# LSTM and sign-weight FFN on one core: reordering the sums of the last part over VectorE, ScalarE and GpSimd

## The chip, the cores and the metric

The kernel runs on one core of a Trainium2 chip. The time is the device time of one launch in microseconds (us), a median over runs. TensorE (PE) multiplies, VectorE (DVE), ScalarE (ACT) and GpSimd (POOL) do the elementwise work, SyncE (SP) issues most DMAs. The engines run their own instruction queues in order and wait for each other by semaphores only.

## The reference, cut to what matters

An LSTM over T = 64 steps, batch 32, input and hidden size 256, feeds an FFN whose weights are +1 or -1; its result is added to x.

```python
xW = einsum('ntd,dg->ntg', x, Wx) + b            # (32, 64, 1024)
for t in range(64):
    a = xW[:, t] + h @ Wh                        # (32, 1024): i, f, o, g
    c = sigmoid(f) * c + sigmoid(i) * tanh(g)
    h = sigmoid(o) * tanh(c)
h = concatenate([hs, -hs], -1)                   # (32, 64, 512)
h = relu(s0 * (h @ w0)) * 2                      # w0: 512 x 1024, +-1
h = relu(s1 * (h @ w1)) * 2                      # w1: 1024 x 1024, +-1
return x + s2 * (h @ w2)                         # w2: 1024 x 256, +-1
```

## The kernel before, in words

The LSTM steps form a serial chain: per step TensorE does 32 small matmuls against the high and low f16 parts of h (lines 485 and 494), VectorE sums the halves (line 1006), ScalarE takes the tanh (line 787), VectorE makes c and h (lines 1012 to 1026), and ScalarE seeds the next step's PSUM (line 676). What TensorE has left in a step is filled with other matmuls: first the input projection (tiles "x"), then the FFN of the steps that are done.

The FFN goes by chunks of steps: chunks 0 to 4 have 8 steps (256 columns), chunks 5 and 6 (N1 and N2) have 12 (384 columns). Layer 0 of chunk c gives eight tiles (0, c, m), layer 1 eight tiles (1, c, m), and the output is a sum over k of products ("o", c, k) in two PSUM banks ACC, one for each half mo. Values are held as a high and a low f16 part, so a drained tile costs one ScalarE operation (the high part, layer_hi) and one VectorE operation (the low part, layer_lo). The layer-1 parts lie in h2, a ring of NH2 = 6. When an output sum is complete, VectorE's y_add (line 860) scales it and adds it into x, and SP sends it out.

Layer 1 of chunks 5 and 6 together is done as a 2 x 2 block product with seven block multiplications instead of eight (Strassen's, in Winograd's form): q = 1 to 7, tiles ("p1", m) to ("p7", m), four m each, eight matmuls each. p2 is accumulated on p1, p6 on p5, p7 on p6, in the same PSUM bank. The weight combinations are mixed by GpSimd inside the loop (line 1078). The input combinations t1 to t4 need chunk 6 and are made behind the loop by n2_terms on VectorE (lines 879 to 884) and term4 on GpSimd (line 1089). Each is split in high (term_hi, ScalarE, line 731) and low part (term_lo: t_lo[0] and t_lo[3] on GpSimd, line 1082; t_lo[1] and t_lo[2] on VectorE, line 888). The product sums are: c11 = p1 + p2; q = p3 + p1, where ScalarE copies p3 out of PSUM (line 736) and GpSimd adds (line 1102); c12 = p6 + q (line 895); c22 = p7 + p1 (line 903); d = c22 - p5 on GpSimd (line 1106) after ScalarE's copy of p5 (line 743); c21 = p4 + d (line 910). c_rest (line 915) makes their low parts and c_split (line 752) the high ones. p7-m takes the bank of p6-m and so waits for c12_sum(m).

The order is written by a planner, make_plan, in Python. tile_order lists the matmuls of the loop in their order; a step t is given a credit fill(t) of 2.2 to 2.3 us, and matmuls are taken from the list by cost until it is spent or one is not ready (its inputs not emptied, or its bank not). act_plan[t] and dve_plan[t] hold what ScalarE and VectorE drain behind step t: VectorE gets at least two tiles a step, more if the planner's time (STEP, CHAIN, LOW, SUM) allows, and at most one y. tail_order puts what is left in order behind the loop. Per step ScalarE does its drains behind the second seed, VectorE behind line 1026.

Of the kernel before, what the change touches and what calls it, by code (L numbers as in the profile page):

```python
# [17 lines left out]
P = 128  # L18
# [4 lines left out]
NH2 = 6  # L23
# [35 lines left out]
STEP, CHAIN, CHAIN_MIN, LOW, SUM, AHEAD, KEEP = 0.87, 2.46, 2.87, 0.33, 0.40, 0.30, 0.05  # L59
# [33 lines left out]

def tile_order():
# [22 lines left out]

def tail_order(left):

    first_outs = [(tile, a) for tile, a in left if tile[0] == "o" and tile[1] == N1]  # L120
    left = [(tile, a) for tile, a in left if (tile, a) not in first_outs]
# [7 lines left out]
    order = [((0, N2, m + 4 * half), a) for m in range(4) for half in (0, 1) for a in range(4)] + left  # L129
    order += [(("p3", m), 2 * k + part) for k in range(4) for m in range(4) for part in (0, 1)]  # L130
    order += products(5, 0, 1) + first_outs + products(6, 0, 1) + products(7, 0, 1) + products(4, 0, 1) + products(5, 2, 3)
    order += outs(N2, 0, 1) + products(6, 2, 3) + outs(N2, 4, 5) + products(7, 2, 3) + outs(N1, 4, 5) + products(4, 2, 3)
    return order + outs(N2, 2, 3, 6, 7) + outs(N1, 6, 7)


def make_plan():
# [3 lines left out]
    pe, act, dve = ([[] for _ in range(T + 3)] for _ in range(3))  # L140
# [6 lines left out]
    ahead, waited = 0.0, 0  # L147

    def ready(tile, a, t):
# [6 lines left out]
        elif tile[0] == "p1":  # L156
            inputs = (0, N1, a // 2) in emptied
        elif tile[0] == "p2":
            inputs = (0, N1, 4 + a // 2) in emptied and ("p1", tile[1]) in emptied
        elif tile[1] == N1:  # L160
            inputs = ("p2", tile[2]) in emptied and ("y", N1 - 1, a // 2) in emptied
        else:
            inputs = (1, tile[1], tile[2]) in emptied
            inputs = inputs and (tile[1] == 0 or tile[2] > 0 or a > 0 or all(("y", tile[1] - 1, mo) in emptied for mo in range(2)))
# [11 lines left out]
    for t in range(-1, T):  # L176
        credit = min(credit, 1.0) + fill(t)
        finished, spent = [], 0.0
        while piece < len(order) and credit > 0.1:
# [3 lines left out]
            if not ready(tile, a, t):  # L183

                later = next((n for n in range(piece + 1, min(piece + AHEAD_O, len(order))) if order[n][0][0] == "o"), 0)
# [28 lines left out]
        for tile, at in finished:  # L214
            if tile[0] in ("x", "p1"):
                emptied.add(tile)
            if tile[0] != "y":
                act[t].append(tile)
# [4 lines left out]
        else:  # L223

            time = ahead + STEP + spent - CHAIN - KEEP - LOW * (t in W2_STEPS)
            lows, ys = ([x for x in todo if (x[0] == "y") == y] for y in (False, True))
            now = lows[:1 if ys and waited else max(2, int(time / LOW))]
            if ys and (len(now) < 2 or len(now) * LOW + SUM <= time):
                now.append(ys[0])
            waited = waited + 1 if ys and ys[0] not in now else 0  # L230
            ahead += STEP + spent - max(CHAIN_MIN, CHAIN + sum(SUM if x[0] == "y" else LOW for x in now))
            ahead = min(max(ahead, 0.0), AHEAD)
        act[t].sort(key=lambda x: x[0] == "x")
# [14 lines left out]
    for tile, a in tail_order(rest):  # L248
        free.sort(key=lambda b: empty_at[b[1]])
        if tile[0] == "o" and tile[1] == N2 and a == 0 and tile[2] == 0:  # L250
# [5 lines left out]
        if a + 1 == matmuls(tile) and tile[0] in (0, 1, "p2", "p3", "p4", "p7"):  # L256
            free.append((bank[tile], tile))
            empty_at[tile] = at + 1.2
            if tile[0] == 0 and tile[1] == N2:
                empty_at[tile] = 2.35 * (tile[2] % 4) + (1.5 if tile[2] < 4 else 3.3)  # L260
    finished = [tile for tile, a in pe[T] if a + 1 == matmuls(tile)]
    act[T] = [x for x in finished if x[0] in (1, "p1", "p2") or x[0] == 0 and x[1] == N1]
    for x in finished:
        if x[0] in (1, "p2") or x[0] == 0 and x[1] == N1:
            dve[T + 1].append(x)
        if x[0] == "o" and x[1] < N1 and x[2] == 7:
            dve[T + 1] += [("y", x[1], mo) for mo in range(2)]
    return pe, act, dve, bank, before


def lstm_ffn(nc, x_d, small_d, wx_d, wh_d, k0_d, k1_d, k2_d, out_d):
    ctx = ExitStack()
    with ctx:
# [26 lines left out]
        h1 = sb("h1", [P, 8192], F16)  # L300
        h2 = sb("h2", [P, NH2, 2, 512], F16)
# [29 lines left out]
        def cut(flat, first, *shape):  # L331
# [19 lines left out]
        h1s = [f.rearrange("p (m a c) -> p m a c", m=8, a=2) for f in (  # L351
            h1[:, 0:4096], h1[:, 4096:8192], h1[:, 0:4096], h1[:, 4096:8192], h1[:, 0:4096])] + [b1]
# [33 lines left out]
        acc_mm, y_made = ([sem(f"{n}{mo}") for mo in range(2)] for n in ("acc_mm", "y_made"))  # L386
# [5 lines left out]
        p3_made, q_made, p5_made, d_made = (sem(n) for n in ("p3_made", "q_made", "p5_made", "d_made"))  # L392
# [755 lines left out]
```

## Time and profile before

| | us |
|---|---|
| median of 3 runs (281.99 to 283.39) | 282.94 |
| profiled execution | 281.88 |
| its span | 279.9 |
| TensorE matmul busy | 269.1 (96%) |
| VectorE busy | 223.2 (80%) |
| ScalarE busy | 173.3 (62%) |
| GpSimd busy | 44.6 (16%) |

The span runs from the first to the last instruction of the profiled execution; the execution's own time also holds what lies around it. Matmul ends in the trace are modelled, so TensorE's busy share is not a share of its peak; starts are better to go by. A line of a timeline gives start, duration, engine, line, output and input, and in brackets how long the engine had been idle and what ended that. Consecutive operations of one engine overlap in part, so that the spacing of starts is shorter than a duration.

### The profile page before, as it was taken

To read this page: it belongs to the slowest core of one execution; us is meant where nothing else is said; L and a number is where in the kernel's file an instruction comes from. 1 tells how busy PE (TensorE), PEld (TensorE's weight loads), DVE (VectorE), ACT (ScalarE), POOL (GpSimd) and SP (SyncE) were. 2 spreads that over 40 slices of the span, in tenths; PEclk is the share of its full clock that TensorE was granted. 3 is DMA by queue.
4 is the path that set the end of the run, shared out by engine and by line. 5 is a ranking of instruction groups with operands and counts; after the bars stand their busy time and mean duration, and the time that the engine had idled before them with its cause. 6 is when DMAs were issued, how large, how long until landed. Compare 5 with 4: busy or idle time off the path is not lost.

```text
span 279.9 us, 8887 instructions
## 1 busy us (share of the span) xinstructions
PE 269.1 (96%) x3568; PEld 218.7 (78%) x3568; DVE 223.2 (80%) x777; ACT 173.3 (62%) x518; POOL 44.6 (16%) x62
## 2 busy tenths in 40 slices
PE   8999999999999999999999999999999996889995
PEld 6788878888999999999999988988878643446662
DVE  3888888888888888888888888878888877947355
ACT  4788887787565666556665565667766667443320
POOL 0110000011221111211112000000000030995030
PEclk9999999999999999999999999999999999999999
DMA  6970000000000000000000000000000000000003
GB/s 207 344 318 1 4 2 0 2 4 2 2 2 4 4 20 20 2 4 18 25 4 2 4 21 21 2 1 22 21 2 2 22 19 0 0 2 0 2 0 112
DMA packets 5432, 8.72 MB, mean 31 GB/s; under 512 B 656, under 2 KB 3472, under 8 KB 5264
## 3 DMA queue, kind: packets, MB, share of 16 engines
q1 hardware_dynamic: 5104, 7.64, 7.8%
q8 instruction: 28, 0.46, 0.6%
q10 hardware_dynamic: 288, 0.52, 0.5%
q14 instruction: 12, 0.10, 0.1%
HBM read 6.07 MB, written 2.10 MB: 29 GB/s over the span
## 4 chain that ended last, share of the span: by engine, by line
PE 72%; DVE 12%; ACT 8%; issue 4%; POOL 3%; DVEq 0%; POOLq 0%; ACTq 0%
PE WK L532 24%; PE WK L515 14%; PE G L494 8%; PE G L485 8%; PE WK L550 5%; PE ACC L564 4%; ACT tT L787 4%; PE G L550 2%; DVE aT L1006 2%; POOL xw L1082 2%; ACT tC L792 2%; DVE h L846 1%; DVE uT L1015 1%; DVE cD L1017 1%; DVE xw L846 1%
## 5 line engine op out<-in xcount | busy, mean ns | idle before, releaser
L532 PE MATMUL WK<-h,k 128*128 128x256 f16 (+1 forms) x848 | 106.3, 276 | 0.4 <-DVE h L1026 0.2
L532 PEld LDWEIGHTS WK<-h,k 128*128 128x128 fp8e5 x848 | 80.1, 98 | 11.7 <-issue 0.6
L787 ACT ACTIVATE tT<-aT 128x128 f32<-128x128 f32 x126 | 38.9, 310 | 49.3 <-DVE aT L1006 48.0
L1006 DVE TENSOR_REDUCE aT<-G 128x128 f32<-128x256 f32 x128 | 48.1, 418 | 4.1 <-PE G L494 2.8
L676 ACT ACTIVATE G<-xw 128x256 f32<-128x256 f32 x126 | 46.6, 370 | 0.0
L515 PE MATMUL WK<-xs,wxs 128*128 128x512 f32 x168 | 42.5, 399 | 0.0
L485 PEld LDWEIGHTS G<-h,w 128*128 128x128 f16 x1008 | 32.1, 96 | 9.6 <-DVE h L1023 8.2
L494 PE MATMUL G<-h,w 128*128 128x64 f16 x1008 | 39.5, 192 | 0.0
L485 PE MATMUL G<-h,w 128*128 128x32 f16 x1008 | 35.2, 177 | 1.1 <-DVE h L1023 1.0
L515 PEld LDWEIGHTS WK<-xs,wxs 128*128 128x128 f32 x168 | 30.4, 188 | 5.9
L494 PEld LDWEIGHTS G<-h,w 128*128 128x128 f16 x1008 | 33.2, 97 | 0.0
L846 DVE SCALAR_TENSOR_TENSOR h<-WK,h 128x256 f16<-128x256 f32 x80 | 30.9, 417 | 0.0
L792 ACT ACTIVATE tC<-cD 128x64 f32<-128x64 f32 x64 | 16.4, 256 | 17.6 <-DVE cD L1017 17.6
L695 ACT ACTIVATE h<-WK 128x256 f16<-128x256 f32 x80 | 26.6, 369 | 0.2
L1023 DVE TENSOR_TENSOR h<-oP,tC 128x64 f16<-128x64 f32 x64 | 14.4, 225 | 13.9 <-ACT tC L792 13.9
L1078 POOL TENSOR_TENSOR mix<-k 128x256 fp8e5<-128x256 fp8e5 x16 | 10.3, 644 | 78.0 <-DVE h L1026 78.0
L564 PE MATMUL ACC<-h,k 128*128 128x256 f16 x160 | 22.7, 273 | 0.0
L1082 POOL TENSOR_TENSOR xw<-w,xw 128x384 f16<-128x384 f32 x8 | 8.5, 1073 | 82.0 <-ACT xw L731 82.0
L1015 DVE SCALAR_TENSOR_TENSOR uT<-tT,cD 128x64 f32<-128x64 f32 x63 | 14.2, 226 | 6.5
L550 PE MATMUL WK<-xw,k 128*128 128x384 f16 x96 | 17.1, 326 | 1.9 <-ACT xw L700 1.9
L668 ACT ACTIVATE xw<-WK,biasS 128x512 f32<-128x512 f32 x28 | 18.1, 678 | 0.4 <-PE WK L515 0.4
L1012 DVE SCALAR_TENSOR_TENSOR vT<-tT 128x64 f32<-128x64 f32 x63 | 14.2, 226 | 2.9
(116 smaller groups left out, 301.8 us busy)
## 6 DMA issues: line engine op xcount, KB each, us to landing
x<-in_x SPq DMA_DIRECT2D x3, 512.0 KB, 8.4
out_y<-x SPq DMA_DIRECT2D x10, 128.0 KB, 1.8
xw<-in_wh SPq DMA_DIRECT2D x4, 256.0 KB, 5.2
k<-in_k SPq DMA_DIRECT2D x1, 1024.0 KB, 10.2
out_y<-x SPq DMA_DIRECT2D x4, 192.0 KB, 1.9
x<-in_x ACTq DMA_DIRECT2D x2, 256.0 KB, 3.4
xw<-in_wx SPq DMA_DIRECT2D x4, 128.0 KB, 4.3
xw<-in_wx SPq DMA_DIRECT2D x2, 256.0 KB, 5.5
```

The source lines that it names most:

```text
L485: eng.matmul(G[g][:, 64 * (j - j0):64 * (j - j0) + B], w16[:, 1, j, k], hi[:, k], start=False, stop=False, skip_group_check=True)
L494: ins = eng.matmul(G[g][:, 64 * (j - j0):64 * (j - j0 + 1)], w16[:, 0, j, k], pair[:, k].rearrange("p a b -> p (a b)"), start=False, stop= ...
L515: ins = eng.matmul(TILE[bank[tile]][:, :], wxs[:, wp, k, j], xs[:, i % 2, xp, k], start=a == 0, stop=a == 5)
L532: ins = eng.matmul(layer_src(tile), w, rhs, start=a == 0, stop=last)
L550: ins = eng.matmul(layer_src(tile), w[:, k, 128 * m:128 * m + 128], rhs[:, k, part], start=a == 0 and q not in (2, 6, 7), stop=a == 7, ski ...
L564: ins = eng.matmul(ACC[mo][:, 0:width(tile)], w2[:, k, 128 * mo:128 * mo + 128], h2[:, k % NH2, part, 0:width(tile)], start=k == 0 and par ...
L676: eng.activation(G[g][:, 0:256].rearrange("p (j h b) -> p j h b", h=2, b=B), src.unsqueeze(2).broadcast_to((P, 4, 2, B)), ACT.Copy, scale= ...
L695: eng.activation(layer_dst(tile, 0), layer_src(tile), ACT.Relu).then_inc(hi_made[layer])
L787: eng.activation(tT[:, B * j0:B * j1], aT[:, j0:j1].rearrange("p j b -> p (j b)"), ACT.Tanh, scale=half_gain0 if t == 0 else half_gain).th ...
L792: eng.activation(tC[:, :, :].rearrange("p j b -> p (j b)"), cD[:, :], ACT.Tanh, scale=0.5).then_inc(c_tanh)
L846: eng.scalar_tensor_tensor(layer_dst(tile, 1), layer_src(tile), 0.0, layer_dst(tile, 0), ALU.max, ALU.subtract).then_inc(lo_made[tile[0]])
L1006: eng.tensor_reduce(aT[:, j0:j1], G[g][:, 0:256].rearrange("p (j h b) -> p j b h", h=2, b=B), op=ALU.add, axis=AX.X).then_inc(added[g])
```

## The change

- t_lo[3] moves from GpSimd to VectorE, and so does q = p3 + p1 (q_sum), which now reads p3 out of PSUM; ScalarE's copy of p3 goes away. t1 and t4 get four slots instead of two, and the waits for their reuse go.
- The output products of chunk 4 (("o", 4, k), 32 matmuls) are no longer in the loop's order but behind it: ten of them first, the others between the layer-0 tiles of chunk 6. The outputs of chunk 5, k = 0 to 3, follow these tiles. h2 has eight places instead of six ring places.
- The output sums of chunks 0 to 3 are scaled and copied out of PSUM by ScalarE (y_copy) and added into x by GpSimd a step later. Chunk 4's are added by VectorE behind the second n2_terms. GpSimd's mixing is put into a loop over the steps.
- The planner has a cost for VectorE by width instead of LOW and SUM, and the last outputs of chunk 5 are ordered by half.

```diff
 def tile_order():
...
-            order += [(("o", c, k), 4) for k in range(6) if at_o[k] == m] + third(c, m)
-
-    order += [(("o", N1 - 1, 6), 4), (("p1", 0), 8), (("o", N1 - 1, 7), 4), (("p1", 1), 8), (("p2", 0), 8), (("p2", 1), 8),
-              (("p1", 2), 8), (("p1", 3), 8), (("p2", 2), 8), (("p2", 3), 8)]
-    return order + [(("o", N1, k), 4) for k in range(4)]
+            if c < N1 - 1:
+                order += [(("o", c, k), 4) for k in range(6) if at_o[k] == m]
+            order += third(c, m)
+
+    return order + [((f"p{q}", m), 8) for q, m in ((1, 0), (1, 1), (2, 0), (1, 2), (2, 1), (1, 3), (2, 2), (2, 3))]
...
 def tail_order(left):
-    order = [((0, N2, m + 4 * half), a) for m in range(4) for half in (0, 1) for a in range(4)] + left
+    others = outs(N1 - 1, *range(8))
+    order = left + others[:10]
+    for k, n in enumerate((6, 8, 8, 0)):
+        order += [((0, N2, k + 4 * half), a) for half in (0, 1) for a in range(4)] + others[:10 + n][10:]
+        del others[10:10 + n]
+    order += outs(N1, 0, 1, 2, 3)
     order += [(("p3", m), 2 * k + part) for k in range(4) for m in range(4) for part in (0, 1)]
-    order += products(5, 0, 1) + first_outs + products(6, 0, 1) + products(7, 0, 1) + products(4, 0, 1) + products(5, 2, 3)
+    order += products(5, 0, 1) + products(6, 0, 1) + products(7, 0, 1) + products(4, 0, 1) + products(5, 2, 3)
     order += outs(N2, 0, 1) + products(6, 2, 3) + outs(N2, 4, 5) + products(7, 2, 3) + outs(N1, 4, 5) + products(4, 2, 3)
-    return order + outs(N2, 2, 3, 6, 7) + outs(N1, 6, 7)
+    order += outs(N2, 2, 3, 6, 7)
+    return order + [(("o", N1, k), 2 * mo + part) for mo in range(2) for k in (6, 7) for part in range(2)]
...
 def make_plan():
-            lows, ys = ([x for x in todo if (x[0] == "y") == y] for y in (False, True))
-            now = lows[:1 if ys and waited else max(2, int(time / LOW))]
-            if ys and (len(now) < 2 or len(now) * LOW + SUM <= time):
-                now.append(ys[0])
+            now = []
+            for x in todo:
+                if len(now) < 2 or sum(map(vector_cost, now + [x])) <= time:
+                    now.append(x)
...
         def _(eng):  # ScalarE
+            def y_copy(tile):
+                _, c, mo = tile
+                e.wait_ge(acc_mm[mo], c + 1)
+                e.wait_ge(signed, 6)
+                e.wait_ge(y_made[mo], c)
+                eng.activation(ty[:, mo], ACC[mo][:, 0:width(tile)], ACT.Copy, scale=FAC).then_inc(y_out[mo])
...
+            for tile in act_plan[T]:
+                empty(tile)
             for k in range(4):
                 n2_relu(k)
                 n2_hi(k)
                 term_hi(0, k)
                 term_hi(1, k)
-            for tile in act_plan[T]:
-                empty(tile)
-            for i, k in ((3, 0), (3, 1), (2, 0), (2, 1), (2, 2), (2, 3), (3, 2), (3, 3)):
-                term_hi(i, k)
-            for m in range(4):
-                p3_copy(m)
+            for i in (2, 3):
+                for k in range(4):
+                    term_hi(i, k)
...
         def _(eng):  # VectorE
+            def q_sum(m):
+                e.wait_ge(prod_mm[3], m + 1)
+                e.wait_ge(p1_made, m + 1)
+                e.wait_ge(t_made[0], 4)
+                eng.tensor_tensor(qs[:, m], layer_src(("p3", m)), p1s[:, m], ALU.add).then_inc(q_made)
...
             for k in range(4):
                 n2_terms(k)
-            for tile in dve_plan[T + 1]:
-                empty(tile)
+                if k == 1:
+                    for mo in range(2):
+                        y_add(N1 - 1, mo)
             for i in (1, 2):
                 for k in range(4):
                     term_lo(i, k)
+            for m in range(4):
+                q_sum(m)
+            for k in range(4):
+                term_lo(3, k)
...
         def _(eng):  # GpSimd
-            for n in range(MIXES):
-                mix_part(n)
+            def y_add(c, mo):
+                at = x[:, mo, steps_of(c)]
+                eng.wait_ge(y_out[mo], c + 1)
+                eng.tensor_tensor(at, at, ty[:, mo], ALU.add).then_inc(y_made[mo])
+
+            for t in range(T):
+                if 0 <= t - MIX_STEP < MIXES:
+                    mix_part(t - MIX_STEP)
+                for _, c, mo in pool_plan[t]:
+                    eng.wait_ge(hl_made, t + 1)
+                    y_add(c, mo)
             for k in range(4):
                 term_lo(0, k)
-                if k >= 1:
-                    term_lo(3, k - 1)
                 term4(k)
-            term_lo(3, 3)
-            for m in range(4):
-                eng.wait_ge(p3_made, m + 1)
-                eng.wait_ge(p1_made, m + 1)
-                eng.tensor_tensor(qs[:, m], qs[:, m], p1s[:, m], ALU.add).then_inc(q_made)
```

## Rows read from the trace of the kernel before

**Rows 1.** Busy by engine from 100 to 200 us: stretch, length, engines, clock, DMA.

```profile
100.00:200.00 100.00, 99.33 (x1645) 89.89 (x1644) 85.27 (x340) 62.44 (x214) 10.91 (x17) 1.00 0.04 13
```

**Rows 2.** Timeline of VectorE's h product, loop steps 16, 40, 43 and 62.

```profile
72.93 0.22 DVE L1023 TENSOR_TENSOR h<-oP,tC 128x64 f16<-128x64 f32 x1 [0.22 <-ACT tC L792]
...
149.46 0.22 DVE L1023 TENSOR_TENSOR h<-oP,tC 128x64 f16<-128x64 f32 x1 [0.22 <-ACT tC L792]
...
159.14 0.22 DVE L1023 TENSOR_TENSOR h<-oP,tC 128x64 f16<-128x64 f32 x1 [0.21 <-ACT tC L792]
...
221.63 0.23 DVE L1023 TENSOR_TENSOR h<-oP,tC 128x64 f16<-128x64 f32 x1 [0.22 <-ACT tC L792]
```

**Rows 3.** Timeline of TensorE's matmuls behind the loop.

```profile
225.88 1.46 PE L532 MATMUL WK<-h,k 128*128 128x384 f16 x8 [0.24 <-DVE h L1026]
...
229.45 0.82 PE L532 MATMUL WK<-h,k 128*128 128x384 f16 x4 [0.17 <-DVE xw L884]
...
231.64 0.82 PE L532 MATMUL G<-h,k 128*128 128x384 f16 x4 [0.69 <-DVE xw L884]
232.30 1.79 PE L550 MATMUL WK<-xw,k 128*128 128x384 f16 x10
236.02 1.47 PE L550 MATMUL WK<-xw,k 128*128 128x384 f16 x8 [1.93 <-ACT xw L700]
...
245.69 0.48 PE L550 MATMUL WK<-xw,mix 128*128 128x384 f16 x2 [2.02 <-POOL xw L1082]
...
250.51 1.48 PE L550 MATMUL WK<-xw,mix 128*128 128x384 f16 x8 [0.45 <-ACT xw L743]
...
253.13 1.46 PE L550 MATMUL WK<-xw,mix 128*128 128x384 f16 x8
```

**Rows 4.** Timeline of VectorE behind the loop.

```profile
227.25 0.56 DVE L879 SCALAR_TENSOR_TENSOR w<-WK,xw 128x384 f32<-128x384 f32 x1 [1.05 <-ACT xw L723]
...
229.44 0.56 DVE L879 SCALAR_TENSOR_TENSOR w<-G,xw 128x384 f32<-128x384 f32 x1
...
235.41 0.55 DVE L884 SCALAR_TENSOR_TENSOR xw<-G,xw 128x384 f16<-128x384 f32 x1
...
238.53 9.89 DVE L888 TENSOR_TENSOR xw<-t,xw 128x384 f16<-128x384 f32 x8
...
252.03 0.56 DVE L895 TENSOR_TENSOR w<-WK,xw 128x384 f32<-128x384 f32 x1 [3.61 <-PE WK L550]
...
276.40 1.14 DVE L860 SCALAR_TENSOR_TENSOR x<-ACC,sc,x 128x384 f32<-128x384 f32 x2 [0.16 <-PE ACC L581]
```

**Rows 5.** Timeline of GpSimd behind the loop.

```profile
228.44 0.92 POOL L1082 TENSOR_TENSOR xw<-w,xw 128x384 f16<-128x384 f32 x1 [74.12 <-ACT xw L731]
...
243.03 1.32 POOL L1089 TENSOR_TENSOR w<-xw,t 128x384 f32<-128x384 f32 x1
...
249.51 3.86 POOL L1102 TENSOR_TENSOR xw<-xw 128x384 f32<-128x384 f32 x4
```

**Rows 6.** Timeline of ScalarE behind the loop.

```profile
248.04 0.52 ACT L731 ACTIVATE xw<-w 128x384 f16<-128x384 f32 x1 [3.12 <-POOL w L1089]
...
249.95 0.51 ACT L743 ACTIVATE xw<-WK 128x384 f32<-128x384 f32 x1
```

**Rows 7.** Timeline of VectorE before the loop, GpSimd idle.

```profile
16.48 2.06 DVE L837 SCALAR_TENSOR_TENSOR w<-xw,sci,w 128x512 f16<-128x512 f32 x3
```

**Rows 8.** Chain of waits (start, duration, what), and one group of lines.

```profile
151.42 0.87 PE ACC L564 x8
...
222.88 0.39 DVE x L860
...
L695 ACT ACTIVATE h<-WK 128x256 f16<-128x256 f32 x80 | 26.6, 369 | 0.2
```

More of the change, by code:

```diff
@@ L91, in cost, with vector_cost @@
     return 0.229 if tile[0] == "x" else 0.000422 * width(tile)
+def vector_cost(tile):
+    return 0.05 + 0.0011 * width(tile)
 def tile_order():
@@ L159, in ready @@
             inputs = (0, N1, 4 + a // 2) in emptied and ("p1", tile[1]) in emptied
-        elif tile[1] == N1:
-            inputs = ("p2", tile[2]) in emptied and ("y", N1 - 1, a // 2) in emptied
         else:
             inputs = (1, tile[1], tile[2]) in emptied
-            inputs = inputs and (tile[1] == 0 or tile[2] > 0 or a > 0 or all(("y", tile[1] - 1, mo) in emptied for mo in range(2)))
+            first = tile[1] > 0 and tile[2] == 0 and a == 0
+            inputs = inputs and (not first or all(("y", tile[1] - 1, mo) in emptied for mo in range(2)))
         return inputs and (before.get(tile) is None or before[tile] in emptied)
@@ L183, in make_plan @@
             if not ready(tile, a, t):
-                later = next((n for n in range(piece + 1, min(piece + AHEAD_O, len(order))) if order[n][0][0] == "o"), 0)
+                instead = ("o", 1) if tile[0] == 0 and a == 0 else ("o",)
+                later = next((n for n in range(piece + 1, min(piece + AHEAD_O, len(order))) if order[n][0][0] in instead), 0)
                 if not later or tile[0] == "o" or not ready(order[later][0], done.get(order[later][0], 0), t):
@@ L249, in make_plan @@
         free.sort(key=lambda b: empty_at[b[1]])
-        if tile[0] == "o" and tile[1] == N2 and a == 0 and tile[2] == 0:
+        if tile == ("o", N2, 0) and a == 0:
             for mo in range(2):
@@ L258, in make_plan @@
             empty_at[tile] = at + 1.2
[L259 to L268, printed above, removed]
+            if tile[0] == 0:
+                empty_at[tile] = 1.6 + 2.2 * (tile[2] % 4) + (1.7 if tile[2] < 4 else 3.4)
+    act[T] = [tile for tile, a in rest if a + 1 == matmuls(tile)]
+    dve[T] += [tile for tile in act[T] if tile[0] != "p1"]
+    return pe, act, dve, pool, bank, before
 def lstm_ffn(nc, x_d, small_d, wx_d, wh_d, k0_d, k1_d, k2_d, out_d):
@@ L349, in lstm_ffn @@
         a11, a21, a12, a22 = (w1[:, 4 * j:4 * j + 4, 512 * i:512 * i + 512] for j in range(2) for i in range(2))
[L351 to L352 removed]
+        h1s = [cut(h1[:, c % 2], 0, 8, 2, B * CHUNKS[c][1]) for c in range(N1)] + [b1]
         G = [pb("G0"), pb("G1")]
@@ L391, in lstm_ffn @@
         t_made, t_hi, t_lo = ([sem(f"{n}{i}") for i in range(4)] for n in ("t_made", "t_hi", "t_lo"))
[L392 removed]
+        q_made, p5_made, d_made = (sem(n) for n in ("q_made", "p5_made", "d_made"))
         c_sum, c_hi, c_lo = ({q: sem(f"{n}{q}") for q in (11, 12, 21, 22)} for n in ("c_sum", "c_hi", "c_lo"))
[L394 to L396 removed]
+        fin_mm, fin_y = ({c: [sem(f"{n}{c}_{mo}") for mo in range(2)] for c in (N1 - 1, N1, N2)} for n in ("fin_mm", "fin_y"))
+        pe_plan, act_plan, dve_plan, pool_plan, bank, before = make_plan()
         def layer_dst(tile, part):
[L399 removed]
+            return h1s[tile[1]][:, tile[2], part] if tile[0] == 0 else h2[:, tile[2], part, 0:width(tile)]
         def layer_src(tile):
@@ L404, in term @@
         def term(i, k):
-            return (t1f[:, k % 2], t23[:, 0, k], t23[:, 1, k], t4f[:, k % 2])[i]
+            return (t1f, t23[:, 0], t23[:, 1], t4f)[i][:, k]
         def steps_of(c):
@@ L456, in _ @@
             eng.dma_start(k2[:, :], k2_d).then_inc(dk2, 16)
-            for c in range(N1):
+            for c in range(N1 - 1):
                 for mo in range(2):
@@ L562, in out_matmul @@
                 elif k == 0:
-                    e.wait_ge(y_made[mo], c)
+                    e.wait_ge(y_out[mo], c)
                 ins = eng.matmul(ACC[mo][:, 0:width(tile)], w2[:, k, 128 * mo:128 * mo + 128],
-                                 h2[:, k % NH2, part, 0:width(tile)], start=k == 0 and part == 0, stop=k == 7 and part == 1)
+                                 h2[:, k, part, 0:width(tile)], start=k == 0 and part == 0, stop=k == 7 and part == 1)
                 if k == 7 and part == 1:
@@ L711, in empty @@
                     p1_copy(tile)
+                elif tile[0] == "y":
+                    y_copy(tile)
                 elif tile[0] == "p2":
```

76 lines of the change are left out of this document (30 added, 46 removed).

## The prediction

> **What bounds the kernel now.** I read the busy time by stretches first, then the starts of the h product, which mark the 64 steps of the loop, then TensorE's timeline behind the loop, and last what VectorE, GpSimd and ScalarE do there. Inside the loop the reader is to see a full TensorE: 99.33 us of matmul in the 100 us from 100 to 200, at a granted clock of 1.00 [rows 1]. The 24 steps between the starts at 72.93 and 149.46 take 76.53 us, 3.19 each; the 19 between 159.14 and 221.63 take 62.49, 3.29 each [rows 2]. So the late steps lose 0.10 us each, 1.9 in all, against the earlier ones that hold the same amount of planned filler.
>
> Behind the loop TensorE is not full. It starts the tail at 225.88, the first half product of group 6 (p6-0) at 250.51 and the first of group 7 (p7-0) at 253.13 [rows 3]; from 250.51 on nothing keeps it waiting until the end. Before 250.51 the waits in front of its rows are 0.24, 0.17, 0.69, 1.93, 2.02 and 0.45 us, 5.5 in all. The first three belong to the layer-0 tiles of the last chunk (hl of the last step, then PSUM banks not yet drained by line 884), the fourth to p2-3, whose bank waits for ScalarE's line 700 copy of p1-3, queued behind the n2 operations; the fifth to t_lo[0] from GpSimd (line 1082); the sixth to ScalarE's copy of p5-0 (line 743).
>
> The last two have one root. GpSimd holds 16 operations in line there: 8 of line 1082, 4 of line 1089, 4 of line 1102. A line-1082 subtraction takes 0.92 us alone, one of line 1089 takes 1.32 while VectorE also works SBUF to SBUF, and the four q sums start only at 249.51 [rows 5]. ScalarE cannot go on to p3 and p5 before GpSimd's last t4: it idles 3.12 us before 248.04 and does p5-0 at 249.95 [rows 6]. VectorE meanwhile takes 9.89 us for eight subtractions of line 888, 1.24 each [rows 4].
>
> **The change, part by part.** The sum goes along TensorE, from the end of the loop's matmuls (225.88 - 0.24 = 225.64) to the start of p6-0, since behind p6-0 the order is the old one.
>
> *Matmuls behind the loop.* Before there were 114 of 384 columns: 32 of the last chunk's layer 0, 18 left of p1 and p2, 32 of p3, 16 of p5, 16 outputs of chunk 5. Sixteen start in 253.13 - 250.51 = 2.62 us, 0.163 each [rows 3]: 18.6 us. With the waits of 5.5 that is 24.1; the rows have 250.51 - 225.64 = 24.9, since a wait is counted from a group's modelled end, 0.16 us behind its last start, five times. After, 32 output matmuls of chunk 4, 256 wide, come in. Eight of those take 0.87 us [rows 8], so 32 take 3.5. The 18 leftovers (2.9 us) should go into the loop, where the 3.5 us of chunk 4's outputs make room: the planner hands out the same credit. Then the tail up to p6-0 is 96 x 0.163 + 3.5 = 19.1 us, and a tail without waits starts p6-0 at 244.8, 5.7 us earlier.
>
> *Do waits come back?* Engine by engine, by the spacings of the rows. Ten chunk-4 output matmuls (1.1 us) run first and cover the last hl; they need nothing of the last step. The first layer-0 tile then starts at 226.75, and VectorE follows 1.37 us behind, as 227.25 follows 225.88 [rows 3, 4]: 228.1. One group of n2 terms takes 2.19 us (229.44 - 227.25). Two end at 232.5; then VectorE waits for the last chunk-4 output. Before that stand 32 x 0.109 + 24 x 0.163 = 7.4 us of matmuls: 233.0. Its two adds at 0.39 [rows 8] end at 233.9, and terms 2 and 3 at 238.3. TensorE puts the other chunk-4 products between the layer-0 tiles, so that each bank has its 2.2 us to drain; the chunk-5 outputs start at 234.3 and need the adds of 233.9; p3 runs 236.9 to 242.1 and needs the last b22 at 238.3. The first four waits, 3.0 us, are covered.
>
> *GpSimd.* Its queue is now t_lo[0] and t4, four times each. The last t1 is ready at about 236.7, its high part at 237.3, so t_lo[0] ends at 238.2 and t4 at 239.2. p5 needs them at 242.1: the wait of 2.02 is gone with 2.9 us to spare. ScalarE, no longer holding the p3 copies, ends term_hi at 241.2 and takes p5-0 (done at 243.4) by 244.1, before 244.8: the wait of 0.45 is gone.
>
> *VectorE inherits the queue.* Between 238.3 and p7-0 it has eight subtractions of line 888, the four q sums out of PSUM, four more subtractions (t_lo[3]) and then c12_sum(0), for which p7-0 waits because it takes p6-0's bank. This is the dear spot. No row shows a 384-wide SBUF-to-SBUF subtraction on VectorE with GpSimd idle. Bounds: 1.24 us, line 888 itself beside GpSimd [rows 4]; and 0.47, the shortest spacing of the n2 operations, from 230 to 235, of which 235.41 is the last [rows 4]. The nearest row is three line-837 operations of 512 columns from SBUF, 2.06 us with GpSimd idle, starts 0.66 apart [rows 7]; by columns alone that is 0.50 for 384. I take 0.53, since part of a duration is fixed, and 0.9 for the first, which meets GpSimd's last t4. So: 238.3 + 0.9 + 7 x 0.53 = 242.9; q sums at 0.49, 244.9; t_lo[3], 247.0; c12_sum(0), 0.56, 247.6. TensorE asks for it at 244.8 + 2.6 = 247.4. A wait of 0.2 to 0.3 comes back. Tail: 5.7 - 0.3 = 5.4 us.
>
> The row first: beside GpSimd line 888 takes 1.24 us, and a sum reading PSUM (252.03) takes 0.56 though GpSimd's q sums run beside it [rows 4, 5]. The Trainium skill, page "SBUF — State Buffer", section "Who interferes with whom", says the same as a rule: VectorE with two SBUF inputs and GpSimd reading SBUF exclude each other for a whole instruction; VectorE with at most one SBUF input is free. Where this speaks against the change is rival two.
>
> *The loop.* Ten y adds of 0.39 us [rows 8] leave VectorE inside the loop (eight go to ScalarE and GpSimd, two behind the loop). Per mean step that is nothing, since TensorE is the limit there; it counts in the late steps, where VectorE's backlog of low parts delays tiles and the chain. Of their 1.9 us [rows 2] I credit 1.0: bounds 0 (the extra belongs to the 384-wide tiles, which stay) and 1.9. The 0.5 us of loop filler less (3.5 - 2.9) is worth 0.2: a step already near its chain length cannot shrink by all of it; bounds 0 and 0.5. The eight added ScalarE copies are 0.37 us each by the 256-wide rows [rows 8] and lie behind the two seeds, where ScalarE idles before the next tanh; cover gone, they would cost 8 x 0.3. GpSimd's adds start behind hl, when VectorE reads PSUM. The mixes keep their steps. The output DMAs of chunk 4 go out at 234 on SP, in front of nothing that waits; below and above zero I see no price. The buffers t1f and t4f with four slots take away waits that no row shows to bind: 0.
>
> *The end.* The last output halves are put so that mo 0 is complete four matmuls before the end, not two. Now both last adds wait in one row, 1.14 us from 276.40 [rows 4]; one of them moves under the matmuls, less 0.3 because the adds overlap in the queue: 0.2 gained; bounds 0 and 0.5.
>
> Sum: 5.4 + 1.0 + 0.2 + 0.2 = 6.8 us. The profiled execution took 281.88 us (span 279.9), so 275.1. The median of the three runs, 282.94, lies 1.06 above it; I forecast 276.1 for the median.
>
> **The rivals.** *One: the loop does not take the leftovers.* The four WK banks and the low parts of chunk 5 can hold p2 back; a step with nothing ready still costs its chain, 3.06 us or so. One product of eight matmuls left over adds 1.3 us behind the loop, and the loop's own 1.2 is not gained: 276.1 + 2.5 = 278.6. For it: such holes are seen in the late steps. Against: the y adds that leave stand in VectorE's queue there, one of them on the chain at 222.88 [rows 8].
>
> *Two: the GpSimd adds meet the h chain.* Lines 1012 to 1026 are VectorE operations with two SBUF inputs. A 256-wide add, two thirds of 0.92, would hold one back by up to 0.6; eight times, 4.8: 280.9. For it: line 888 beside GpSimd. Against: an add that starts right behind hl ends before the next vT, some 1.4 us later; only two adds behind a mix reach it. The skill's rule ("the loser fully blocks", page "SBUF — State Buffer") gives this same case.
>
> *Three, slower: the subtraction costs VectorE 1.24 us by itself*, GpSimd or not. Then 238.3 + 8 x 1.24 + 2.0 + 4 x 1.24 + 0.56 = 255.7 for c12_sum(0), and p7-0 starts 2.6 us later than before; less the 1.4 of loop and end, 282.94 + 1.2 = 284.1. It decides from 1.14 us a piece. For it: each of the eight is slow, and its second input is f16. Against: GpSimd was busy beside nearly all of them, and line 837, f16 output, is not slow.
>
> *Four: something between*, 0.8 us a piece: p7-0 late by 3.3 more, 279.4.
>
> **How the numbers follow.** Forecast 0.62; one 0.18; two 0.07; three 0.06; four 0.07. Left open at either side, the range 274.0 to 279.8 holds the forecast's own band, one and four. No change within 0.5% (1.4 us, about what a measurement of this kernel tells) means 281.5 to 284.4: part of three and the upper edge of two, 0.05; slower 0.05; faster 0.90.
>
> **What would show it.** p6-0 near 243.5 and no TensorE wait over 0.5 us between the loop's end and it; line 888 at about 0.55 to 0.6 us once GpSimd's t4 is done; GpSimd done with t4 before p3 ends; c12_sum(0) within 0.5 us of p6-0's end; late steps at 3.2 us. Wrong if line 888 stays above 1 us with GpSimd idle, if p2 matmuls stand in front of the chunk-4 outputs behind the loop, or if the h chain's lines grow beside the new adds.

## The result, and the profile after

The changed kernel takes 275.89 us (median of 4 runs, 275.60 to 276.26); the kernel before, on the same chips, 282.63 (4 runs, 281.99 to 283.39). The ratio is 0.976, with a 95% interval from 0.973 to 0.979: faster, by 6.7 us. The forecast was 276.1, with a range of 274.0 to 279.8.

The profiled executions took 281.88 and 275.96 us, 5.9 apart; the spans 279.9 and 274.2. All splits below are made inside the spans.

The medians lie further apart (6.7) than the profiled executions (5.9). Part of that goes with TensorE's clock. The kernel before was run 32 more times beside the experiments. In 11 of these runs the granted clock, averaged over the span, was 1.00, and the times are 281.80 to 282.67 us (median 282.26); in 12 it was 0.992 to 0.994, and the times are 282.74 to 283.37 (median 283.00). All four runs of the changed kernel show 1.00. So some 0.4 us (282.63 - 282.26) of the 6.7 go with a clock that only the kernel before lost. Its profiled execution is one with a clock of 1.00, so no trace shows where it was lost.

First the page of the profile after: busy time (share of the span, instructions) and the shares of the chain of waits.

```profile
PE 268.8 (98%) x3568; PEld 219.2 (80%) x3568; DVE 219.3 (80%) x777; ACT 174.3 (64%) x522; POOL 40.7 (15%) x62
...
PE 85%; DVE 7%; ACT 5%; DMA 1%; issue 1%; ACTq 0%
```

TensorE is as busy as before, 268.8 us against 269.1, in a span 5.7 us shorter. The work is nearly the same and idle time is gone. The next view is TensorE's timeline behind the loop (start, busy time, line, count, and in brackets any wait ahead of the row). It answers to [rows 3].

```profile
225.90 1.26 PE L565 MATMUL ACC<-h,k 128*128 128x256 f16 x10
226.99 1.46 PE L533 MATMUL WK<-h,k 128*128 128x384 f16 x8
228.29 0.82 PE L565 MATMUL ACC<-h,k 128*128 128x256 f16 x6
...
234.59 2.76 PE L582 MATMUL ACC<-h,k 128*128 128x384 f16 x16
237.19 0.81 PE L551 MATMUL WK<-xw,mix 128*128 128x384 f16 x4
...
242.39 7.80 PE L551 MATMUL WK<-xw,mix 128*128 128x384 f16 x47
```

No row carries a bracket. The chunk-4 outputs (128x256, line 565) stand first and between the layer-0 tiles. The last row, cut at 250, holds 47 of the 48 matmuls of the first halves of p5, p6 and p7, without a break, where the kernel before waited 2.02 us for GpSimd and 0.45 for ScalarE. Sixteen matmuls of p5 at 0.163 put p6-0 at 242.39 + 2.61 = 245.00. From the end of the loop's matmuls to p6-0 the kernel before needed 250.51 - 225.64 = 24.9 us; this one needs 245.00 - 225.90 = 19.1, which is 5.8 less.

The engines that feed it come next: VectorE (answers to [rows 4]), then the single rows of GpSimd and ScalarE (to [rows 5, 6]).

```profile
233.28 0.88 DVE L862 SCALAR_TENSOR_TENSOR x<-ACC,sc,x 128x256 f32<-128x256 f32 x2 [0.41 <-PE ACC L565]
...
238.32 4.66 DVE L885 TENSOR_TENSOR xw<-h,xw 128x384 f16<-128x384 f32 x8
242.90 1.01 DVE L891 TENSOR_TENSOR xw<-WK,xw 128x384 f32<-128x384 f32 x2
...
244.76 1.95 DVE L885 TENSOR_TENSOR xw<-w,xw 128x384 f16<-128x384 f32 x4
246.63 0.54 DVE L898 TENSOR_TENSOR t1f<-WK,xw 128x384 f32<-128x384 f32 x1
```

```profile
238.32 1.43 POOL L1097 TENSOR_TENSOR w<-xw,h 128x384 f32<-128x384 f32 x1
```

```profile
243.89 0.49 ACT L746 ACTIVATE xw<-WK 128x384 f32<-128x384 f32 x1 [2.56 <-PE WK L551]
```

VectorE's eight subtractions (line 885, line 888 before) take 4.66 us instead of 9.89. GpSimd's last t4 ends at 239.75, well ahead of p5 at 242.39. ScalarE, which idled for GpSimd before, now waits for TensorE alone and has p5-0 copied at 244.4, before p6-0 starts.

The loop, by TensorE's first group of line 486 and by the start of VectorE's h product (line 1026; the first and the second pair answer to those of [rows 2]):

```profile
19.49 0.56 PE L486 MATMUL G<-hz,w 128*128 128x32 f16 x16
```

```profile
73.23 0.23 DVE L1026 TENSOR_TENSOR h<-oP,tC 128x64 f16<-128x64 f32 x1 [0.22 <-ACT tC L795]
...
150.36 0.22 DVE L1026 TENSOR_TENSOR h<-oP,tC 128x64 f16<-128x64 f32 x1 [0.22 <-ACT tC L795]
...
160.04 0.22 DVE L1026 TENSOR_TENSOR h<-oP,tC 128x64 f16<-128x64 f32 x1 [0.22 <-ACT tC L795]
...
222.88 0.22 DVE L1026 TENSOR_TENSOR h<-oP,tC 128x64 f16<-128x64 f32 x1 [0.22 <-ACT tC L795]
```

The 24 early steps take 77.13 us (76.53 before), the 19 late ones 62.84 (62.49 before). The loop is no faster: from that first group to the tail it is 225.90 - 19.49 = 206.41 us, against 206.43 before, where the same group (then line 485) started at 19.21. The 0.28 us by which the loop starts later is in no edit; it differs from run to run (19.00 and 19.57 in two experiments with the same code there).

This zero hides two things that cancel. The last group of this line marks the last step, first after, then before:

```profile
223.25 0.56 PE L486 MATMUL G<-h,w 128*128 128x32 f16 x16
```

```profile
222.33 0.55 PE L485 MATMUL G<-h,w 128*128 128x32 f16 x16
```

From the first group to the last it is 203.76 us, against 203.12 before: 0.64 longer. From the last group to the tail it is 2.65 us, against 3.31, because the plan gives the last step 11 filler matmuls instead of 14. (The 225.64 of the kernel before is a modelled end. By the spacing of the starts it lies 0.16 us earlier, which would move 0.16 us of gain from the loop to the tail.)

At the end, the last matmuls and the last adds:

```profile
269.69 1.46 PE L582 MATMUL ACC<-h,k 128*128 128x384 f16 x8
```

```profile
270.63 1.18 DVE L862 SCALAR_TENSOR_TENSOR x<-ACC,sc,x 128x384 f32<-128x384 f32 x2
```

The adds end 271.81 - 271.15 = 0.66 us behind the matmuls; before it was 0.85. So the span's 5.7 us are 5.8 (tail) + 0.0 (loop) + 0.2 (end) - 0.3 (the later start).

### The profile page after: what moved, and what is told of

It is laid out like the page before. It is cut to its first block, busy times and chain, and to the rows that moved or that the text cites. A ratio compares the mean times of both kernels' runs of the same rounds, so it can differ in the third digit from the quotient of the medians.

```text
span 274.2 us, 8895 instructions
## 1 busy us (share of the span) xinstructions
PE 268.8 (98%) x3568; PEld 219.2 (80%) x3568; DVE 219.3 (80%) x777; ACT 174.3 (64%) x522; POOL 40.7 (15%) x62
## 4 chain that ended last, share of the span: by engine, by line
PE 85%; DVE 7%; ACT 5%; DMA 1%; issue 1%; ACTq 0%
PE WK L533 27%; PE WK L516 14%; PE G L495 10%; PE WK L551 9%; PE G L486 9%; PE ACC L565 6%; PE G L551 4%; PE WK L582 2%; ACT tT L790 2%; DVE aT L1009 2%; PE ACC L582 1%; DMA x<-in_x 1%; PE G L516 1%; DVE xw L848 1%; ACT xw L688 1%; PE ACC L516 1%
## 5 line engine op out<-in xcount | busy, mean ns | idle before, releaser
L533 PE MATMUL WK<-h,k 128*128 128x256 f16 (+1 forms) x856 | 107.7, 276 | 0.0
L565 PE MATMUL ACC<-h,k 128*128 128x256 f16 x160 | 22.0, 273 | 0.0
L565 PEld LDWEIGHTS ACC<-h,k 128*128 128x128 fp8e5 x160 | 15.3, 98 | 2.1
```

What stands on the lines that cost most here:

```text
L533: ins = eng.matmul(layer_src(tile), w, rhs, start=a == 0, stop=last)
L565: ins = eng.matmul(ACC[mo][:, 0:width(tile)], w2[:, k, 128 * mo:128 * mo + 128], h2[:, k, part, 0:width(tile)], start=k == 0 and part == 0 ...
```

## The experiments

Two questions: what makes the tail's 5.8 us, and why the loop gives nothing. The ratio is against the kernel before, run beside it. The diffs are cut to what matters; three dots stand for lines left out.

| kernel | median us | ratio, 95% interval |
|---|---|---|
| changed kernel | 275.89 | 0.976 (0.973 to 0.979) |
| e1_queue_back | 284.37 | 1.006 (1.004 to 1.008) |
| e10_queue_back_warm | 281.70 | 0.997 (0.996 to 0.998) |
| e2_split_alone | 279.09 | 0.988 (0.986 to 0.990) |
| e11_pool_busy | 283.82 | 1.005 (1.003 to 1.008) |
| e9_t0_on_vector | 276.77 | 0.979 (0.977 to 0.980) |
| e4_y_on_vector | 276.27 | 0.979 (0.977 to 0.981) |
| e5_y_spread | 274.99 | 0.974 (0.972 to 0.975) |
| e6_lag | 275.74 | 0.976 (0.974 to 0.978) |
| e7_spread_lag | 274.88 | 0.973 (0.972 to 0.975) |
| e12_spread_lag2 | 274.34 | 0.971 (0.970 to 0.973) |

### The order without the split: e1_queue_back

The changed kernel with the last part's queues as before: t_lo[3] and the q sums on GpSimd, the p3 copies on ScalarE.

```diff
 VectorE:
-            for m in range(4):
-                q_sum(m)
-            for k in range(4):
-                term_lo(3, k)
...
 ScalarE:
+            for m in range(4):
+                p3_copy(m)
...
 GpSimd:
                 term_lo(0, k)
+                if k >= 1:
+                    term_lo(3, k - 1)
                 term4(k)
+            term_lo(3, 3)
+            for m in range(4):
...
+                eng.tensor_tensor(qs[:, m], qs[:, m], p1s[:, m], ALU.add).then_inc(q_made)
```

> The changed kernel with one part undone: t_lo[3] and the q sums are GpSimd's again, with ScalarE's copy of p3; the outputs of chunk 4 stay behind the loop. Theory A (the two parts of the tail need each other): GpSimd's queue ends its last t_lo[0] at about 245.6 us as before, p5 waits some 2.5 us for it, and ScalarE's copy of p5-0 lies behind the p3 copies at about 250, with no chunk-5 outputs left to cover it; p6-0 starts near 250.3 instead of 245.0 and the time is 281.2 (280.5 to 281.9), so nearly the whole gain is gone. Rival B (the parts add up): only the waits of 2.02 and 0.45 us before p5 and p6 come back, 278.4 us. Rival C (the gain is the order alone): 276 us.

Measured 284.37, slower than the kernel before and above all three forecasts. TensorE's timeline of this run:

```profile
245.90 2.84 PE L551 MATMUL WK<-xw,mix 128*128 128x384 f16 x10 [2.38 <-POOL xw L1094]
...
250.74 8.29 PE L551 MATMUL WK<-xw,mix 128*128 128x384 f16 x32 [2.00 <-ACT xw L751]
```

Both old waits are back and the second is longer (2.00 for 0.45), because the matmuls that used to stand between p5 and p6 (chunk 5's first outputs) now run earlier. That is the expected part (p6-0 at 250.74, forecast 250.3). What theory A missed is in the stretches (length, then busy time of PE, PEld, DVE, ACT, POOL, then the granted clock as the number ahead of the last two):

```profile
244.00:245.00 1.00, 0.00 (x0) 0.00 (x0) 1.00 (x2) 0.40 (x1) 1.00 (x2) 1.00 0.00 0
...
247.00:248.00 1.00, 1.00 (x5) 0.48 (x4) 0.36 (x1) 0.00 (x0) 1.00 (x1) 0.50 0.00 0
...
255.00:256.00 1.00, 1.00 (x5) 0.49 (x4) 0.00 (x0) 0.00 (x0) 0.00 (x0) 0.50 0.00 0
...
257.00:258.00 1.00, 1.00 (x8) 0.61 (x7) 0.88 (x3) 0.20 (x1) 0.00 (x0) 1.00 0.00 0
```

After the idle time the granted clock is 0.50 (1.2 GHz) and five matmuls run in a microsecond; at 257 it is 1.00 (2.4 GHz) again, with eight. The kernel before, behind its wait of 2.02 us at the same place, shows no such fall in its profiled execution:

```profile
246.00:247.00 1.00, 1.00 (x9) 0.60 (x7) 1.00 (x1) 0.00 (x0) 1.00 (x2) 1.00 0.00 0
```

### The same with TensorE kept busy: e10_queue_back_warm

```diff
             def matmul(tile, a):
+                if tile == ("p5", 0) and a == 6:
+                    warm_up(("p5", 1), 22)
+                if tile == ("p6", 0) and a == 0:
+                    warm_up(("p4", 0), 12)
...
```

warm_up issues that many 256-wide matmuls of zeros into the bank that the named tile fills later.

> The kernel with GpSimd's queue put back (284.37 us), with 22 matmuls of zeros, 256 wide, in the wait ahead of p5's last part and 12 in the wait ahead of p6-0, each into a PSUM bank that is free; they keep TensorE at work and release nothing. Theory F (about 3 us of that kernel's loss are TensorE at half its clock, granted 0.50 from about 246.5 to 256.4, after an idle stretch of 2.38 us): the clock stays 1.00 and the time is 281.3 (280.8 to 281.9). Rival G (the loss is waits alone): 284.4 or more.

Measured 281.70. The stretch from 240 to 260 us, at a clock of 1.00, and the timeline of TensorE:

```profile
240.00:260.00 20.00, 18.42 (x124) 11.64 (x122) 13.61 (x18) 8.58 (x19) 15.18 (x14) 1.00 0.00 1
```

```profile
243.28 2.56 PE L612 MATMUL WK<-zero 128*128 128x256 f16 x22
...
249.17 1.48 PE L612 MATMUL WK<-zero 128*128 128x256 f16 x12 [1.54 <-ACT xw L753]
250.69 5.37 PE L551 MATMUL WK<-xw,mix 128*128 128x384 f16 x32
```

p6-0 starts at 250.69, as in e1 (250.74), and its 32 matmuls take 5.37 us instead of 8.29. So 2.7 us of e1 are the clock (284.37 - 281.70, by the medians; e1's runs differ, with mean clocks of 0.982 and 0.994), and the queues as they were cost 281.70 - 275.89 = 5.8 us by their waits alone.

### The split without the order: e2_split_alone

The kernel before, with only the engines changed: VectorE takes t_lo[3] and the q sums (straight from PSUM), ScalarE loses the p3 copies, and the buffers of t1 and t4 get four slots.

> The kernel before with one part of the change: t_lo[3] and the q sums on VectorE, t1 and t4 with four slots, no p3 copies; order, planner and y adds are those of before. Theory A: the bank waits behind the loop (0.17, 0.69, 1.93 us) stay, the waits of 2.02 and 0.45 us go, p6-0 starts near 247.8 instead of 250.5: 2.7 us less than before, about 280.0 (279.4 to 280.6). Rival B (only the order counts): 282.6. Rival C (the engine split is the whole gain): under 278.

Measured 279.09, 0.3 below theory A's range; the rivals are refuted. TensorE's rows that answer to [rows 3]:

```profile
226.42 1.46 PE L536 MATMUL WK<-h,k 128*128 128x384 f16 x8 [0.25 <-DVE h L1027]
...
236.57 1.47 PE L554 MATMUL WK<-xw,k 128*128 128x384 f16 x8 [1.94 <-ACT xw L704]
...
248.28 1.46 PE L554 MATMUL WK<-xw,mix 128*128 128x384 f16 x8
```

and VectorE's subtractions, which answer to line 888 of [rows 4]:

```profile
239.08 3.83 DVE L883 TENSOR_TENSOR xw<-t,xw 128x384 f16<-128x384 f32 x8
```

The waits behind GpSimd are gone and those of the last chunk's banks stay (1.94 for p2-3). From first tail matmul to p6-0 it is 21.9 us, 24.6 before. The eight subtractions take 3.83 us where they took 9.89: 0.47 each with GpSimd idle. So the split alone is worth 3.4 us by the ratio, of which the tail up to p6-0 shows 2.8; some of the rest is the clock again, which was 1.00 in all four runs of e2. The rest of the change without the split loses (e1), or gains 0.3% where the clock is kept up (e10), and both together bring 6.7. The order needs the split, for it takes away the products that covered GpSimd's queue.

### GpSimd kept busy: e11_pool_busy

The changed kernel, with ten 384-wide SBUF-to-SBUF adds on GpSimd behind the last t4, whose results nobody reads.

```diff
+            for n in range(10):
...
+                eng.tensor_tensor(k0[:, 1, 0:NW].bitcast(F32), p1s[:, 0], p1s[:, 1], ALU.add).then_inc(mixed)
```

> The changed kernel with ten more 384-wide adds on GpSimd, SBUF to SBUF, behind its last t4; nothing waits for them. Theory H (a VectorE subtraction with two SBUF inputs takes 0.47 us alone and about 1.24 beside GpSimd): VectorE's eight subtractions take 9.5 us instead of 4.6, the q sums out of PSUM stay at 0.47, c12_sum(0) comes near 253.3 instead of 246.6 and p7-0 waits 5 to 6 us; with the clock lost after such a gap 283 to 285.5 us. Rival I (VectorE's line 888 was slow before for another reason): 275.9.

Measured 283.82, as theory H has it. VectorE, GpSimd and TensorE of this run:

```profile
238.09 9.46 DVE L885 TENSOR_TENSOR xw<-h,xw 128x384 f16<-128x384 f32 x8
247.47 1.01 DVE L891 TENSOR_TENSOR xw<-WK,xw 128x384 f32<-128x384 f32 x2
```

```profile
239.48 12.53 POOL L1117 TENSOR_TENSOR k<-xw 128x384 f32<-128x384 f32 x10
```

```profile
253.42 4.36 PE L551 MATMUL WK<-xw,mix 128*128 128x384 f16 x16 [5.89 <-DVE t1f L898]
```

The subtractions are back at 1.18 each, while the sums that read PSUM keep their 1.01 for two. GpSimd's adds take 1.25 each, against 0.96 for its four q sums with VectorE idle (3.86 in [rows 5]). The price of 1.24 in [rows 4] is thus GpSimd's work beside VectorE, not the subtraction's own. The Trainium skill, page "SBUF — State Buffer", section "Who interferes with whom", has as a rule that a VectorE instruction with two SBUF inputs contends with a GpSimd instruction that reads SBUF, and that one with at most one SBUF input does not. The trace agrees with both halves: 1.18 against 0.47 us for the subtractions, and 1.01 for two of the sums that read PSUM here as in the changed kernel.

### How near VectorE's queue is: e9_t0_on_vector

```diff
 VectorE:
-            for i in (1, 2):
+            for i in (0, 1, 2):
                 for k in range(4):
                     term_lo(i, k)
...
 GpSimd:
-                term_lo(0, k)
```

> The changed kernel with the four t_lo[0] subtractions moved from GpSimd to VectorE too, ahead of its others. Theory J (VectorE's queue behind the loop is the nearest next bound: c12_sum(0) ends at 247.2 us, p7-0 starts at 247.6, some 0.45 us of room): four times 0.47 us more, less 0.4 for the first subtraction that no longer meets GpSimd, make c12_sum(0) 1.5 us later and p7-0 1.0 to 1.1 us later: 276.9 us (276.5 to 277.4). Rival K (VectorE has room for 2 us): 275.9.

Measured 276.77, 0.9 us more, as theory J has it. The intervals of the ratios touch, but its four runs (276.38 to 277.18) lie above the four of the changed kernel. TensorE:

```profile
248.79 2.77 PE L551 MATMUL WK<-xw,mix 128*128 128x384 f16 x16 [0.64 <-DVE t1f L898]
```

p7-0 now waits for c12_sum(0), the place that the prediction called the dear spot. Four more subtractions (1.9 us, less GpSimd's interference with the first one) turn a small margin into a wait of 0.64.

### The loop: e4_y_on_vector

The changed kernel with the y adds of chunks 0 to 3 back on VectorE inside the loop.

```diff
-            if tile[0] == "y":
-                pool[t + 1].append(tile)
-            act[t].append(tile)
+            if tile[0] != "y":
+                act[t].append(tile)
...
```

> The changed kernel with the y sums of chunks 0 to 3 undone: VectorE adds them out of PSUM inside the loop again, with the new planner costs; nothing else is different. Theory A (moving them off VectorE cost time): the long steps 27 and 36 (vT held back beside GpSimd's adds, 0.2 us each beyond the filler) and 53 (seven ScalarE operations ahead of the tanh, 0.7 us) go, a half-full step at 44 comes: 275.2 us (274.7 to 275.7). Rival B (as predicted, the move is worth about 1 us in the late steps): 276.9. Rival C: no difference, 275.9.

Measured 276.27, ratios 0.979 and 0.976 with overlapping intervals: by the medians the move is worth 0.4 us, less than rival B's 1 us, and theory A, that it costs time, is refuted. By the steps of the profile it does take something away. The extra time of a step is here its length less its planned filler and 0.865 us. Over the loop it sums up to 6.4 us in e4 and 5.7 in the changed kernel, of which 0.03 a step, some 1.9, stands in steps without any loss. The kernel before has 5.0, and the places differ: before, steps 45, 51 and 58 mostly (0.57, 0.47, 0.53); after, steps 27 (0.22), 36 (0.26) and 53 to 60 (0.71 in 53). Old losses went, new ones came. The changed kernel's rows show three causes.

In step 27 (and 36), two GpSimd adds behind a mix:

```profile
105.85 0.64 POOL L1088 TENSOR_TENSOR mix<-k 128x256 fp8e5<-128x256 fp8e5 x1 [2.52 <-DVE h L1029]
106.45 1.41 POOL L1102 TENSOR_TENSOR x<-x,t1f 128x256 f32<-128x256 f32 x2
```

```profile
103.95 0.23 DVE L1015 SCALAR_TENSOR_TENSOR vT<-tT 128x64 f32<-128x64 f32 x1
...
107.22 0.72 DVE L1015 SCALAR_TENSOR_TENSOR vT<-tT 128x64 f32<-128x64 f32 x1
```

vT, on the h chain, takes 0.72 instead of 0.23. In step 53 the chain waits for ScalarE instead:

```profile
190.73 0.87 ACT L723 ACTIVATE t1f<-ACC,sc 128x256 f32<-128x256 f32 x2
```

```profile
191.83 0.23 DVE L1015 SCALAR_TENSOR_TENSOR vT<-tT 128x64 f32<-128x64 f32 x1 [0.74 <-ACT tT L790]
```

Both y copies stand behind five other ScalarE operations and ahead of the step's tanh (tT). In e4 the same step loses 0.8 us, because both y adds stand on VectorE ahead of the reduction aT:

```profile
190.88 0.87 DVE L861 SCALAR_TENSOR_TENSOR x<-ACC,sc,x 128x256 f32<-128x256 f32 x2
191.66 0.75 DVE L1010 TENSOR_REDUCE aT<-G 128x128 f32<-128x256 f32 x2
```

So the move of the y adds carried the obstruction of this step from one engine to the other. In steps 55 to 60 the cause is the chain of waits (start, duration, engine, what):

```profile
203.26 0.41 ACT xw L688
203.67 0.39 ACT xw L694
204.06 0.02 issue
204.08 0.56 DVE xw L848
204.64 0.34 DVE aT L1009
```

VectorE has no backlog there any more, so it takes the low part of a layer-0 tile (line 848) in the step in which ScalarE makes its r1 copy and high part (688, 694), and the reduction aT of the h chain stands behind it. In the plan of the kernel before VectorE drained these tiles a step after ScalarE. That lag is gone in e4 too, where steps 55 to 59 have the same extra time as after, 1.5 us. So it is the new order and the planner's new costs that took it away, and not the move of the y adds; no run separates these two from each other.

### The y work spread over steps: e5_y_spread

```diff
-                pool[t + 1].append(tile)
-            act[t].append(tile)
+                pool[t + 2 + tile[2]].append(tile)
+                act[t + 1 + tile[2]].append(tile)
+            else:
+                act[t].append(tile)
```

> The changed kernel with the two y sums of a chunk spread over two steps: the copy of half 0 is ScalarE's one step later, that of half 1 two steps later, GpSimd's adds a step behind each. Theory A: one add (0.71 us) behind a mix (0.64) ends before the next vT, so vT stays at 0.23 us in all steps, and step 53 loses its overfull ScalarE: 1.0 us less than the changed kernel, 274.9 us (274.5 to 275.4). Rival B (the two-add steps are hidden by TensorE's filler): 275.9.

Measured 274.99, 0.9 us less than the changed kernel, as expected. The intervals of the ratios overlap, but all five runs (274.47 to 275.23) lie below the four of the changed kernel. The same spot as above in this run:

```profile
109.25 0.72 POOL L1104 TENSOR_TENSOR x<-x,t1f 128x256 f32<-128x256 f32 x1
```

```profile
109.90 0.23 DVE L1017 SCALAR_TENSOR_TENSOR vT<-tT 128x64 f32<-128x64 f32 x1
```

One add a step ends before vT starts and vT keeps its 0.23. The extra time falls from 5.7 to 4.7 us; step 53 from 0.71 to 0.14.

### VectorE one step behind: e6_lag, e7_spread_lag and e12_spread_lag2

e6 lets VectorE drain chunk 5's layer-0 tiles a step later; e7 is e5 and e6 together.

```diff
-                (late if spent - at < 0.75 else todo).append(tile)
+                (late if spent - at < 0.75 or tile[:2] == (0, N1) else todo).append(tile)
```

> The changed kernel with one change in the planner: VectorE drains the layer-0 tiles of chunk 5 a step later than ScalarE, as its old backlog did, not in the same step. Theory D (the steps 55 to 60 are 0.13 to 0.37 us longer than their filler because VectorE waits for ScalarE's high part of the same step and its reduce comes late): these extras go, 1.2 to 1.5 us less than the changed kernel, 274.5 us (274.1 to 275.0); two steps get less full. Rival E (the two 384- and 256-wide drains by themselves make the chain that long): 275.9.

> Both corrections together: the y sums spread over two steps (measured alone at 274.99 against 275.89 us) and the one-step lag of VectorE for chunk 5's layer 0. Theory D: their gains add up, 273.6 us (273.1 to 274.2). Rival E: 275.0, as with the spread alone.

Both missed what theory D forecast: 275.74 and 274.88, the same as without the lag (275.89 and 274.99). The wait itself went (the extra of steps 55 to 59 fell from 1.5 to 0.6 us), but the banks were now released a step later in the plan. The planner found none for steps 53 and 59 and filled them with 1.73 instead of 2.21 us, and with 1.94; step 53 then ran 1.20 us beyond its filler. e12 is e7 with the lag only from the third tile of the chunk on.

```diff
+ ... or tile[:2] == (0, N1) and tile[2] >= 2 ...
```

> The changed kernel with the y sums spread over two steps and VectorE's one-step lag only from tile 2 of chunk 5's layer 0 on, so that step 53 keeps its full filler. Theory L (the lag's gain was lost because the planner, not finding a bank, filled steps 53 and 59 less): half of the lag's 0.9 us comes through, 274.5 us (274.2 to 274.9). Rival M (what a shorter chain frees is always given back as less filler): 274.95, as with the spread alone.

Measured 274.34, within theory L's range: less than the changed kernel, with intervals that just don't touch, and the lowest of all here, though its runs overlap with those of e5 and e7; the extra is 4.2 us. That ScalarE makes the high part before the r1 copy, the other way to shorten that wait, was not tried.

## Why the prediction held, and where it did not

*The tail* was forecast at 5.4 us and brought 5.8. Its waits went as the prediction has it: the chunk-4 outputs cover the last hl and the four bank waits; GpSimd was done with t4 at 239.75 (forecast 239.2); p5-0 was copied at 244.4 (244.1), before p6-0 at 245.0 (244.8). e10 prices the engine split within the new order at 5.8 us, e2 within the old order at 3.4. One sign that the prediction gives, p6-0 near 243.5, is at odds with its own sum, 244.8; the sum was right, and by the sign as written the tail would have failed.

*The mis-sized term there* is the subtraction on VectorE: I took 0.53 us a piece, the runs show 0.47 (4 in 1.95 from 244.76; 8 in 3.83 in e2). The lower bound, the shortest spacing of the n2 operations, was the price. For the first eight this did not show, by luck: the one that met GpSimd's last t4 started at 238.79 and held the next up until 240.09, 1.30 us where I took 0.9, and that made up for seven at 0.47 in place of 0.53 (the eight are done at 242.90, forecast 242.9). The q sums and the last four ran as fast as the lower bound. So c12_sum(0) comes at 246.63 rather than 247.0, and the wait of 0.2 to 0.3 us that I subtracted before p7-0 does not exist. e9 shows that the spot was the right one to worry about.

*The loop step failed.* It said that ten y adds leaving VectorE would give back 1.0 of the late steps' 1.9 us, and the lighter filler 0.2. Measured for both: 0.0. The lighter filler gave more than was credited, for nearly all of it came in the last step: three matmuls fewer, 0.5 us. The y part gave nothing: up to the last group the loop is 0.64 us longer than before, and the late steps take 3.31 us each instead of the 3.2 named as the sign. The losses of steps 45 and 51 did go, and that of 58 fell from 0.53 to 0.28. In their place came the three waits of e4's section. With the y adds back on VectorE (e4) it is longer still, 204.47 us from the first group to the last against 203.76, so the move itself does help, by 0.4 us in the medians; that is less than what the new order and the planner's costs take. I had named two of their conditions and priced them at nothing: "the eight added ScalarE copies lie behind the two seeds, where ScalarE idles before the next tanh" is not so in step 53, where both copies and five more operations meet; and rival two is true in steps 27 and 36, for 0.5 us instead of 4.8, by just the exception written into it (two adds behind a mix). There vT, a line of the h chain, grew beside the new adds, which the prediction names as a sign of being wrong. The third, a wait that VectorE's lag of a step had hidden, I had not seen; I had asked only what the y adds leaving would free, and not what the new plan would do to the chain. Had the copies been a step apart (e5), 0.9 of the 1.2 us would have come.

*The end* gave the 0.2 forecast.

*The sum* came out near for a reason that is not its own. In profiled time the forecast was 275.1 and the measurement 275.96: the 1.2 us of the loop and the 0.3 of the start are missing, 0.4 of tail is over, and 0.2 came outside the span. To that I added 1.06 us for the distance from the profiled execution to the median, a distance that the changed kernel does not have (275.89 against 275.96). In the kernel before most of it goes with the granted clock of the runs, as said with the result. That offset, not the working, closed the gap, and it was luck.

*The rivals.* One (leftovers behind the loop): refuted; the plan leaves none, and the p2 matmuls right ahead of the chunk-4 outputs are the last step's filler. Two (the adds meet the h chain): true in two steps only, as said. Three and four (a dear subtraction): refuted by e2 and e11.

## What to carry to other kernels

Behind a loop, draw every engine's queue on one time axis, and reorder the matmuls and the helpers' queues together: here either half alone brought half the gain or a loss. Unloading an engine that is not the bound pays only where its queue was the wait. Look for what its lag hid, spread the moved work over steps, and count filler only where the planner has a bank for it. And before adding the distance between one profiled run and a median to a forecast, ask what makes that distance and whether the changed kernel will have it.

## What the runs showed of the hardware

- The granted clock fell to 0.50 behind an idle time of TensorE of 2.38 us, some 0.6 us after it had resumed (e1), and during one of 5.89 us, some 2.3 us into it (e11). In the profiled executions it stayed at 1.00 behind the 2.02 us of the kernel before [rows 3] and behind 1.54 in e10. In e1 it was 0.50 from about 246.5 to 256.7, although matmuls ran through most of that. There the clock cost 2.7 us beyond the waits (e10).
- The same kernel can keep or lose the clock from run to run: of 32 runs of the kernel before 11 show a mean of 1.00 and 12 one of 0.992 to 0.994, and their medians are 0.7 us apart.
- A 384-wide f32 subtraction from SBUF to SBUF on VectorE: 0.47 us apart alone (e2), 1.18 (e11) to 1.24 (before) beside GpSimd, whose own adds go from 0.96 [rows 5] to 1.25 (e11). A sum with one input in PSUM stays at 0.5 either way (line 891 in e11 and after). Even the 64-wide vT goes from 0.23 to 0.72 where it meets a 256-wide add (after).
